# A second LayerNorm pass split around two divisions, and two statistics moved behind a residual

## The reference

```python
for l in range(N_LAYERS):                       # 6
    q = (x @ Wq[l] + bq[l]); k = (x @ Wk[l] + bk[l]); v = (x @ Wv[l] + bv[l])   # 16 heads of 16
    a = causal_linear_attn(feature_map(q), feature_map(k), v)
    x = x + (a @ Wo[l] + bo[l])
    x = layer_norm(x, g1[l], be1[l])
    y = gelu(x @ W1[l] + b1[l]) @ W2[l] + b2[l]         # 256 -> 1024 -> 256
    x = layer_norm(x + y, g2[l], be2[l])
```

## Time and profile before

| what | value |
|---|---|
| device time, median of 3 runs | 1846.03 us (1843.54 to 1850.28) |
| profiled execution, device time | 1842.59 us |
| its span, first to last instruction | 1840.8 us |
| TensorE busy | 1681.1 us, 91% |
| VectorE busy | 1391.5 us, 76% |
| ScalarE busy | 915.6 us, 50% |
| GpSimd busy | 697.6 us, 38% |
| mean granted TensorE clock | 0.969 |

### The profile page before, as it was taken

How to read it: one execution, slowest core, us unless ns; L and a number is a source line. 1 busy time by engine, 2 the same in 40 slices (tenths; PEclk the granted TensorE clock), 3 DMA queues, 4 the chain that set the end, 5 groups by cost and what they waited for, 6 DMA issues and landing times. The chain is left out here.

```text
span 1840.8 us, 39590 instructions
## 1 busy us (share of the span) xinstructions
PE 1681.1 (91%) x16726; PEld 1368.0 (74%) x16726; DVE 1391.5 (76%) x2741; ACT 915.6 (50%) x1455; POOL 697.6 (38%) x521
## 2 busy tenths in 40 slices
PE   5899999999999999999999999999688898886795
PEld 4688887888888888888888888888566666664432
DVE  5777878888888879888888888876667777775245
ACT  2354555454545454455554545444356656654343
POOL 2343455344544445334544435433302222222122
PEclk8899999999999999999999999999889999999797
DMA  5100001000010001100010000100000000000001
GB/s 112 47 2 30 7 27 30 2 30 10 24 30 3 28 10 27 27 30 10 25 30 2 30 10 25 20 1 2 23 13 13 15 16 13 8 2 1 14 0 46
DMA packets 43071, 36.53 MB, mean 20 GB/s; under 512 B 14224, under 2 KB 41360, under 8 KB 42896
## 3 DMA queue, kind: packets, MB, share of 16 engines
q1 hardware_dynamic: 42896, 34.01, 6.8%
HBM read 31.91 MB, written 2.10 MB: 18 GB/s over the span
## 5 line engine op out<-in xcount | busy, mean ns | idle before, releaser
L630 POOL TENSOR_TENSOR e_h_lo<-e_h_f,e_h_hi 128x512 fp32r<-128x512 f32 x192 | 249.2, 1300 | 342.1 <-ACT e_h_hi L490 339.7
L715 DVE TENSOR_TENSOR e_am<-e_sc,c_amask 128x1024 f32<-128x1024 f32 x192 | 225.8, 1217 | 16.9 <-PE e_sc L365 16.5
L489 ACT ACTIVATE e_h_f<-e_pr,e_h_bias 128x512 f32<-128x512 f32 x192 | 132.3, 689 | 212.5 <-PE e_pr L166 208.5
L1407 DVE TENSOR_REDUCE x_mx<-x_psS 128x4 f32<-128x1024 f32 x128 | 155.9, 1223 | 48.0 <-PE x_psS L1094 48.0
L164 PE MATMUL e_pr<-e_yT_hi,e_W_hi 128*128 128x512 f32 x384 | 169.3, 441 | 0.3 <-DVE e_yT_lo L708 0.3
L1256 ACT ACTIVATE x_ex<-x_psT 128x1024 f32<-128x1024 f32 x128 | 131.1, 1024 | 71.0 <-PE x_psT L1123 71.0
L164 PE MATMUL e_tr<-e_W_hi,e_h_hi 128*128 128x256 f32 x576 | 164.3, 285 | 1.4 <-issue 1.4
L166 PE MATMUL e_tr<-e_W_hi,e_h_lo 128*128 128x256 f32 x576 | 162.6, 282 | 0.0
L165 PE MATMUL e_tr<-e_W_lo,e_h_hi 128*128 128x256 f32 x576 | 162.1, 282 | 0.0
L166 PE MATMUL e_pr<-e_yT_hi,e_W_lo 128*128 128x512 f32 x384 | 154.0, 401 | 0.0
L165 PE MATMUL e_pr<-e_yT_lo,e_W_hi 128*128 128x512 f32 x384 | 153.9, 401 | 0.0
(11 more groups left out here) (279 smaller groups left out, 4961.3 us busy)
## 6 DMA issues: line engine op xcount, KB each, us to landing
e_raw_m<-in_L_attn_W_dram SPq DMA_DIRECT2D x12, 1024.0 KB, 7.2
x_ctok<-in_ctx_dram SPq DMA_DIRECT2D x8, 256.0 KB, 2.7
x_xo<-in_x_dram SPq DMA_DIRECT2D x8, 256.0 KB, 2.8
out_dram<-X SPq DMA_DIRECT2D x4, 512.0 KB, 2.9
e_raw_a<-in_L_attn_Wq_dram SPq DMA_DIRECT2D x6, 256.0 KB, 5.1
e_raw_a<-in_L_attn_Wk_dram SPq DMA_DIRECT2D x6, 256.0 KB, 5.5
e_raw_a<-in_L_attn_Wv_dram SPq DMA_DIRECT2D x6, 256.0 KB, 6.3
e_raw_a<-in_L_attn_Wo_dram SPq DMA_DIRECT2D x6, 256.0 KB, 6.5
```

The costliest lines, as they stand in the source:

```text
L489: act.activation(h_f[:, m % HR, :], ps_pr[m % 2][:, :], ACT.Gelu, bias=h_bias[:, m:m + 1])
L630: pool.tensor_tensor(h_lo[:, m, :], h_f[:, m % HR, :], h_hi[:, m, :].bitcast(F32), ALU.subtract).then_inc(h_lo_done, 1)
L715: dve.tensor_tensor(am[:, s % 2, c, :, :, :], ps_sc[:, :, c * 2 * P:(c + 1) * 2 * P].rearrange("p r (h n) -> p r h n", n=P), amask[:, :].u ...
L1407: dve.tensor_reduce(mx[:, N % 2, :, :].rearrange("p i (h a x) -> p h a i x", h=2, a=2)[:, pair, :, :, 0], ps_s[pair][:, :, :].rearrange("p ...
```

## The change

Two edits of VectorE's order, in the second norm of the encoder. No instruction is added or taken away.

- The second pass of chunks 0 and 1 stays ahead of the third division; that of chunks 2 and 3 now follows the fourth division, ahead of `aT_lo`.
- The statistics of chunks 0 and 1 stood between the second and the third residual; now the third residual follows the second, and the three statistics follow it, ahead of the key-value product.

In the step u = 23, without attention, the two halves of the second pass follow each other as before.

```diff
-            def scale(i, n, tile, bias):
+            def scale(i, n, tile, bias, parts=range(SB)):
                 dve.wait_ge(rs_done[i], n + 1)
-                for s in range(SB):
+                for s in parts:
                     x = X[:, tile * SB + s, :]
                     dve.wait_ge(xc_done[i], SB * n + s + 1)
                     dve.scalar_tensor_tensor(x, x, rs[i][:, s:s + 1], bias[:, :], ALU.mult, ALU.add).then_inc(ln_done[i], 1)
...
                 if prev:
                     residual(2, 1, d, last, m_full, xb2_done)
-                    spread(2, 0, d, last)
-                    spread(2, 1, d, last)
                     residual(2, 2, d, last, m_full, xb2_done)
-                    spread(2, 2, d, last)
+                    for s in range(SB - 1):
+                        spread(2, s, d, last)
...
                     if prev and s == 2:
-                        scale(2, d, last, rows_m["be2"])
+                        scale(2, d, last, rows_m["be2"], range(0, 2))
                     if attn:
                         divide(s)
+                    if prev and s == SB - 1:
+                        scale(2, d, last, rows_m["be2"], range(2, SB))
```

## The result

The changed kernel took 1816.5 us, the median of 4 runs (1815.31 to 1820.20), against 1848.15 us for the kernel before (4 runs, 1843.54 to 1850.73). The ratio is 0.9839, with a 95% interval of 0.9813 to 0.9864. Forecast was 1818, in a range of 1811 to 1832. The profiled execution took 1815.39 us, forecast 1814.7.

What follows compares the result with a forecast made beforehand. TensorE, busy nine tenths of the span, was taken to bound the kernel. Savings of 8.3 + 10.9 + 5.4 + 3.3 = 27.9 us take the profiled 1842.59 us to 1814.7, the median to 1818.1; range 1811 to 1832.

Steps and rivals of the forecast that it cites:

- The split frees the third division: L397's waits for the third division go: 1.67 us in five q, k, v steps, 2.17 in five W2 steps.
- The turns: VectorE passes alternate with GpSimd subtractions, 1.40 us per pass; the first moved pass is held by the MLP's sixth piece.
- The cover of the moved half: Behind the fourth division, VectorE's wait for ScalarE hides the two moved passes: cost nothing, cover thin, 0.15 to 0.25 us.
- The rival in which the moved half is late in every step: Second moved pass also held by the seventh piece: 1.14 us in 22 steps costs 25.1, giving 1843; chance 0.07.
- The clock: Half-clock stretches after the 2.17 us waits in five W2 steps go with the waits: 5 x 1.08 = 5.4 us.
- the last rival: Late moved half at L257 also drops the clock in each of 22 steps: costs 48.8 us, giving 1867; chance 0.03.
- The statistics: Moved behind the third residual, they cut L327's wait by 0.66 us in five W2 steps: 3.3; delayed key-value product free.
- The sum: All savings together, 27.9 us: profiled time 1814.7 us, median 1818.1; chance 0.74.
- both moved passes lose to a piece in every step: Strict reading of the shared-port rule for VectorE and GpSimd behind the fourth division: sum ends near the time of before.

Runs made afterwards that it cites:

- e1: The split of the second pass alone, statistics in the old order, against the kernel before: 1821.56 us, ratio 0.9858.
- e2: The statistics' move alone on the kernel before, second pass whole and ahead of the third division: 1845.70 us, ratio 0.9986.
- e3: The change with three passes ahead of the third division and one behind the fourth: 1823.67 us, ratio 0.9865 to the kernel before.
- e4: The kernel before, with GpSimd's weight subtractions moved from ahead of the MLP's fifth piece to ahead of its seventh: 1824.26 us, ratio 0.9869.
- e5: The change with one pass ahead of the third division and three behind the fourth: 1822.19 us, ratio 0.9868 to the kernel before.
- e6: The change with all four passes behind the fourth division: 1848.59 us, ratio 1.0017 to the kernel before.
- e8: The change again, unaltered, timed beside the later experiments on the same chip: 1818.44 us, ratio 0.9848 to the kernel before.

## Why the prediction was right, point by point

**The split frees the third division** (8.3 + 10.9 forecast). Right, and shown by e1 alone. Both terms are a little small: the q, k, v steps gave 9.2 us, and a W2 step without its half-clock stretch is 53.6 us in e2, a plain step 51.3, so the 2.17 us wait cost about 2.3. The likely reason is how the row counts: a matmul's record is 0.40 us long while the next starts after 0.23, and idle time begins at the record's end. That is argued from the rows, not tried by itself.

**The turns.** Right in kind: e3's third pass cost 1.44 us, and e4 took the subtractions away and had 1.66 for four. I had forecast that the first moved pass would be held by the sixth piece in the plain step. It went first, 0.07 us ahead of it, and the second was held: 1.89 us for two, ending 0.46 before the low part starts. I had forecast 0.25 for this. I had let the pass start at the end of the division's record; it starts 0.08 us before that end (563.57 against 563.23 + 0.42), and that put it first.

**The cover of the moved half.** Right, but with nothing to spare in the W2 steps. A cover of 0.15 us was forecast there, and none was found that can be measured, so that this part came out right by less than the records resolve. e5 and e6 show what stood behind it: a third pass behind the fourth division costs 1.2 us in each W2 step, a fourth costs 1.27 us in every other step. The rival in which the moved half is late in every step was priced about rightly (25.1 us; e6 lost 30.2), and its condition was not met.

**The clock** (5.4 us forecast). The kernel before had the stretch after all five of its 2.17 us waits, the change had none, e4 removed them by another road and e3 by a shorter wait. That the stretches go with the wait is shown. The price was about right: 1.0 in e2, and in the change a W2 step gained 3.37 us, of which the wait makes 2.3. Two details were off. A wait of that length does not always bring a stretch: three of five in e2, three of five after 1.72 us in e6. And between the first and the second slow stretch lies one 1.67 us wait (at 417.13), not two as the prediction says; the reading holds all the same, since none of the five such waits in that trace has a stretch behind it. Against the last rival, a clock that drops in every step, that was an argument from five waits. e6 is the test: the half is late in every step, and none of its 16 waits of 1.56 us dropped the clock. It ran in 1848.59 us, not in 1867.

**The statistics** (3.3 us forecast). Right by the trace: L327 lost 3.2 us in the change and 3.3 in e2, and the later key-value product cost no wait. By the timing it was not told apart from nothing.

**The sum.** 27.9 forecast; 29.2 in the steps concerned, 27.2 in span and in profiled time. That the profiled time came within 0.7 us of the forecast is in part luck: the 1.3 us more from the steps, the 1.6 of the head and the 3.6 of the later blocks nearly cancel. The difference of the medians was 31.7 in the first timing and 27.1 in e8's. The parts that the change doesn't touch vary by several us, enough for that.

## What to carry to other kernels

Ask of each wait of the bounding engine what stands in front of its releaser in that engine's queue, and split there: half of the work was enough, since the wait was shorter than half. Then ask what the moved half meets in its new place. Here it met another engine's subtractions, and in the W2 steps two passes just fitted, with nothing to spare, where three did not. And see whether a wait is followed by a stretch of low clock: removing it may be worth a half more than its row says.

## What the runs showed of the hardware that I had not expected

- The turns go both ways. In the plain step after, VectorE's pass starts at 563.57, 0.07 us ahead of GpSimd's subtraction; the subtraction then takes 1.54 us in place of 1.28, and the two passes 1.89. The Trainium skill (SBUF — State Buffer, Who interferes with whom) calls the shared ports an exclusive lock and has the order of issue decide who blocks. These rows agree. The prediction had read out of that page that both moved passes lose to a piece in every step. In the plain step the first one issued ahead of the piece and did not lose; in the W2 steps both were held, and still the low part was on time.
- A half-clock stretch came after three of five waits of 1.72 us at L257 and after three of five of 2.17 us at L397 in e2, but after all five of 2.17 us in the kernel before, and after none of 16 waits of 1.56 us in e6 or of five of 1.5 us in e5. The length of the wait alone does not decide; what does stays open.
- The two blocks behind the encoder, whose code is the same in every kernel here, lasted from 599.0 to 607.4 us. A change worth 3 us can't be read from the span; it has to be read from the steps it touches.
